# Starting the routed-expert stage in the middle of a shared-expert block

## The chip, the cores and the metric

The kernel runs on one core of a Trainium2 chip. The metric is the device time of one execution in microseconds. The engines are TensorE (PE in the profile, its weight loads PEld), VectorE (DVE), ScalarE (ACT), GpSimd (POOL) and SyncE (SP), which only issues DMAs.

## What is computed

4096 tokens (2 x 2048) of 512 features go through one layer: layer norm, a cross attention in which the scores are used only to pick 15 delays of the values, a residual, a second layer norm, and a feed-forward network with 16 experts of which each token uses 4, plus a shared expert of hidden width 1024. Only the feed-forward part is touched here:

```python
sg = xf @ shared_gate_w.T
su = xf @ shared_up_w.T
shared_out = silu(sg) * su @ shared_down_w.T
topk_idx, w, _ = _route(xf, router_w, correction_bias)      # 4 of 16 experts
combine = zeros((S, E)).at[arange(S)[:, None], topk_idx].add(w)
g = einsum('sc,ech->esh', xf, gate_w)
u = einsum('sc,ech->esh', xf, up_w)
hw = silu(g) * u * combine.T[:, :, None]
routed = einsum('esh,ehc->sc', hw, down_w)
return shared_out + routed
```

## The kernel before, in words

Every float32 matrix is split in a high and a low float16 part, and a product is three float16 products (high x high, high x low, low x high).

**The shared expert** works on 8 blocks of 512 tokens (four tiles of 128) and on 8 chunks of 128 hidden units, so there are 64 chunks, numbered g = 8 k + c for block k. A chunk is 24 matrix products of 512 columns for gate and up (`shared_half`, L948, or `gate_up_at`, L1137) and 12 for down (`shared_down`, L964, or `down_at`, L1149), which add up in four PSUM banks over the chunks of a block. Between them stand, per chunk, a silu on ScalarE (L1339, L1430), a product on VectorE from PSUM (L1623, L1961), the high part on ScalarE (L1345) and the low part on VectorE (L1629, L1966). The down products of a chunk come one chunk later in TensorE's order. After the last chunk of a block, VectorE adds the four PSUM banks to x1, the layer's residual (`shared_sum`, L1644, or `sum_at`, L1976); the down products of the next block wait for it.

**Stage A** runs chunks 0 to 39 (`FIRST = 5` blocks). Beside it the routing is worked out, the routed weights are split, and a list of tokens by expert is made: for each of the 32 tiles of tokens VectorE makes a one-hot of rows (L1858, one instruction for 4 experts) and four one-hots of blocks (L1861, one instruction each), in a ring of four buffers, and TensorE multiplies them (`tokens`, L980, four products a tile). The table `HOT` says which tiles belong to which of the chunks 26 to 37 (two or three each). The low parts of the 16 routed weights are made by GpSimd (`routed_weights_lo`, L2050 and L2051), one behind each conversion on ScalarE (`CONVERT`, L1351 to L1354), the last in chunk 37. When the token list is there (`s_tok`), GpSimd copies its first column (L2063) and begins to gather token rows (L2070).

**Stage B**, the routed experts, is a list of 143 blocks of 128 tokens of one expert. Its gate and up products are L1074, the turned hidden units L1088, the down products L1098, and each block's result goes to memory (`y_dram`). It begins with `turn_rows` (L1057) of the first two gathered blocks. Beside it SyncE saves x1 of block 4, loads x1 of block 5 and the turned rows of block 6 (the tables `OUT_AT`, `IN_AT`, `QUARTER_AT`).

**Stage C** runs chunks 40 to 63, and beside them the combination: for each of the 32 tiles GpSimd gathers 4 x 128 rows of `y_dram` (L2127, 128 gathers in a ring of four tiles, paced by `PACE`, 20 groups of 12 products for 37 gathers), VectorE multiplies and adds each (L1953, in the numbers of `PARTS_AT` per chunk) and SyncE writes the tile out. SyncE loads what the tiles need by the tables `OLD_IN`, `X1_IN` and `TURN_IN`; it takes its work strictly in order.

Of the kernel before, what the change touches and what calls it, by code (L numbers as in the profile page):

```python
# [26 lines left out]
F32 = mybir.dt.float32  # L27
# [5 lines left out]
P = 128  # L33
# [6 lines left out]
SH = HS // H  # L40
# [18 lines left out]
FIRST = 5  # L59
SPLIT = E // (FIRST - WITH)  # L60
# [22 lines left out]
RING = 4  # L83
PACE = (20, 37)
# [58 lines left out]
def build(nc, x, ctxT, wk, wqT, wv, wo, biases, bo, cb, routerT, gu_w, dn_w, const, const_r, out):  # L143
    with ExitStack() as ctx:
# [85 lines left out]
        old = [view(o + 8 * KB * (RING + k), [TB, D]) for k in range(FIRST)]  # L230
        xt_end = view(o + 88 * KB, [2 * KC, BLK], F16)
        x1_end = {FIRST: x1b, **{k: view(o + 8 * KB * (RING + k - 1), [TB, D]) for k in range(FIRST + 1, NB)}}
# [62 lines left out]
        x1s_dram = nc.dram_tensor("x1s_dram", [FIRST, P, TB, D], F32)  # L295
# [68 lines left out]
        s_hot, s_hot_used, s_tok = sem("one_hot_ready"), sem("one_hot_used"), sem("tokens_ready")  # L364
        s_token_now = sem("tokens_copied")
# [4 lines left out]
        s_xq = {k: sem(f"xt_quarters_in{k}") for k in (FIRST + 1, FIRST + 2)}  # L370
# [20 lines left out]
        for k, olds in enumerate(OLD):  # L391
            turns += [(FIRST + k, (FIRST + k) * TB + t) for t in range(TB)]
            turns += [(FIRST + k, m) for m in range(sum(OLD[:k]), sum(OLD[:k + 1]))]
        of_block = [[n for n, (k, m) in enumerate(turns) if k == FIRST + b] for b in range(len(OLD))]

        def result(m):

            return old[m // TB][:, m % TB, :] if m < FIRST * TB else x1_end[m // TB][:, m % TB, :]
# [16 lines left out]
        def gate_up_bank(s, n):  # L415

            return bank[(6 if isinstance(s, int) and s < 2 else 2) + n % 2]

# [10 lines left out]
        def _(sp):  # L429
# [200 lines left out]
            def x1s_tile_out(k, t):  # L630
                sp.wait_ge(s_x1s, TB * k + BANKS_FREE.index(t) + 1)
                sp.dma_start(x1s_dram[k][:, t, :], x1b[:, t, :]).then_inc(s_x1sw, 16)

            def x1_tile_in(k, t):
                sp.dma_start(x1b[:, t, :], x1_rows[k][:, t, :]).then_inc(s_x1i, 16)

# [6 lines left out]
            sp.wait_ge(s_sd, FIRST * SH)  # L643
            turn_fourth(1, 1)
            for s in range(BLOCKS):
# [3 lines left out]
                if s in OUT_AT:  # L649
                    x1s_tile_out(FIRST - 1, OUT_AT.index(s))  # L650
                if s in IN_AT:
                    if s == IN_AT[0]:
                        sp.wait_ge(s_x1sw, 16 * (FIRST - 1 + TB))
                    x1_tile_in(FIRST, IN_AT.index(s))
# [1523 lines left out]
```

## Time and profile before

| | us |
|---|---|
| time, median of 3 runs | 1013.74 (1006.69 to 1016.24) |
| the profiled execution's own time | 1004.85 |
| its span | 1003.0 |
| TensorE busy | 985.6 |
| VectorE busy | 660.1 |
| GpSimd busy | 437.1 |
| ScalarE busy | 380.6 |

The rows further down all come from the one profiled execution, whose own time is 1.85 us over its span and 8.9 us below the median of the runs. "Busy" of TensorE is the union of overlapping matrix products, so that a short pause between two of them doesn't show. A bracket at the end of a timeline row is the idle time ahead of it and what ended it; "issue" stands for nothing that the profile shows, "remote" for an unknown queue or another core.

### The profile page before, as it was taken

To read this page: it belongs to the slowest core of one execution; us is meant where nothing else is said; L and a number is where in the kernel's file an instruction comes from. 1 tells how busy PE (TensorE), PEld (TensorE's weight loads), DVE (VectorE), ACT (ScalarE), POOL (GpSimd) and SP (SyncE) were. 2 spreads that over 40 slices of the span, in tenths; PEclk is the share of its full clock that TensorE was granted. 3 is DMA by queue.
4 is the path that set the end of the run, shared out by engine and by line. 5 is a ranking of instruction groups with operands and counts; after the bars stand their busy time and mean duration, and the time that the engine had idled before them with its cause. 6 is when DMAs were issued, how large, how long until landed. Compare 5 with 4: busy or idle time off the path is not lost.

```text
span 1003.0 us, 21036 instructions
## 1 busy us (share of the span) xinstructions
PE 985.6 (98%) x6750; PEld 601.2 (60%) x6750; DVE 660.1 (66%) x1534; ACT 380.6 (38%) x776; POOL 437.1 (44%) x508
## 2 busy tenths in 40 slices
PE   9999999999999999999999999999999999999997
PEld 7776744444444444446787777878778744344442
DVE  4977688874588898875455554555545436676767
ACT  3646454433544333223444444444444411111111
POOL 0726422131145222134545444454454167776774
PEclk9999999999999999999999999999999999999999
DMA  9736858878463611416999999999888578988776
GB/s 347 259 121 206 293 182 233 227 206 237 156 179 99 200 62 63 144 35 178 265 269 256 271 267 256 255 269 249 243 242 252 173 210 267 309 272 283 242 239 219
DMA packets 176636, 219.02 MB, mean 218 GB/s; under 512 B 101225, under 2 KB 112361, under 8 KB 175529
## 3 DMA queue, kind: packets, MB, share of 16 engines
q1 hardware_dynamic: 152792, 139.05, 46.6%
q0 software_dynamic: 23760, 78.79, 26.0%
q8 instruction: 61, 1.00, 0.4%
q14 instruction: 23, 0.18, 0.1%
HBM read 124.72 MB, written 70.27 MB: 194 GB/s over the span
## 4 chain that ended last, share of the span: by engine, by line
PE 87%; DVE 5%; issue 3%; DMA 2%; ACT 2%; another core or an unknown queue 0%; POOL 0%; DVEq 0%; SPq 0%; ACTq 0%; POOLq 0%
PE bank L1074 19%; PE bank L948 18%; PE bank L1137 11%; PE bank L964 9%; PE bank L1098 9%; PE bank L1149 5%; PE bank L1057 5%; PE bank L723 2%; PE bank L703 2%; PE bank L1088 2%; PE bank L800 1%; DMA arena<-in_dn_w 1%; PE bank L980 1%; PE bank L713 1%; PE bank L807 1%
## 5 line engine op out<-in xcount | busy, mean ns | idle before, releaser
L948 PE MATMUL bank<-arena 128*128 128x512 f16 x960 | 218.1, 379 | 0.2 <-ACT arena L1330 0.2
L1074 PE MATMUL bank<-arena 128*128 x1716 | 211.2, 273 | 1.0 <-DVE arena L1615 0.8
L1074 PEld LDWEIGHTS bank<-arena 128*128 128x128 f16 x1716 | 162.9, 98 | 26.9 <-issue 2.0
L2070 POOL DMA_INDIRECT arena<-xr_dram,arena x143 | 140.7, 984 | 57.7 <-issue 45.9
L2127 POOL DMA_INDIRECT arena<-y_dram,arena x128 | 134.4, 1050 | 70.9 <-issue 32.9
L948 PEld LDWEIGHTS bank<-arena 128*128 128x128 f16 x960 | 94.2, 99 | 108.2 <-ACT arena L1330 0.7
L1137 PE MATMUL bank<-arena 128*128 128x512 f16 x576 | 129.2, 379 | 1.6 <-issue 1.5
L1098 PE MATMUL bank<-arena 128*128 x429 | 115.4, 378 | 0.5 <-ACT arena L1408 0.5
L1345 ACT ACTIVATE arena<-arena 128x512 f16<-128x512 f32 x64 | 40.3, 629 | 197.8 <-DVE arena L1623 96.0
L1890 DVE SCALAR_TENSOR_TENSOR arena<-bank,arena 128x128 f32<-128x128 f32 x143 | 41.6, 291 | 107.6 <-ACT arena L1397 82.8
L1953 DVE SCALAR_TENSOR_TENSOR arena<-arena 128x512 f32<-128x512 f32 x128 | 95.1, 750 | 25.4 <-DMA arena<-y_dram,arena 16.9
L964 PE MATMUL bank<-arena 128*128 128x512 f16 x480 | 110.1, 379 | 0.2 <-DVE arena L1629 0.2
L1137 PEld LDWEIGHTS bank<-arena 128*128 128x128 f16 x576 | 56.1, 98 | 71.0 <-issue 4.6
L2050 POOL TENSOR_TENSOR arena<-arena 128x1024 f32 x16 | 34.5, 2158 | 144.6 <-ACT arena L1354 144.6
L1397 ACT ACTIVATE arena<-bank 128x128 f32<-128x128 f32 x143 | 39.7, 278 | 142.8 <-PE bank L1074 92.1
L1408 ACT ACTIVATE arena<-bank 128x512 f32<-128x512 f32 x143 | 83.2, 582 | 2.9 <-PE bank L1098 1.7
L2063 POOL COPY arena<-arena 128x1 int32 (+1 forms) x143 | 28.4, 198 | 121.1 <-PE bank L1057 108.7
L964 PEld LDWEIGHTS bank<-arena 128*128 128x128 f16 x480 | 46.8, 98 | 56.5 <-DVE arena L1629 0.7
L1893 DVE TENSOR_TENSOR arena<-arena 128x128 f16<-128x128 f32 x143 | 41.9, 293 | 53.7 <-ACT arena L1401 47.7
L1615 DVE COPY arena<-bank 128x1024 f16<-128x1024 f16 x108 | 73.7, 682 | 5.0 <-issue 2.6
L1057 PEld LDWEIGHTS bank<-arena 128*128 128x128 f16 x864 | 57.1, 97 | 26.1 <-DMA arena<-xr_dram,arena 0.9
L1149 PE MATMUL bank<-arena 128*128 128x512 f16 x288 | 66.1, 379 | 5.6 <-DVE arena L1976 2.9
(226 smaller groups left out, 1281.7 us busy)
## 6 DMA issues: line engine op xcount, KB each, us to landing
y_dram<-arena SPq DMA_DIRECT2D x143, 256.0 KB
arena<-in_x SPq DMA_DIRECT2D x8, 1024.0 KB, 12.4
xr_dram<-arena SPq DMA_DIRECT2D x16, 512.0 KB, 3.8
x_dram<-arena SPq DMA_DIRECT2D x8, 1024.0 KB, 5.6
arena<-in_gu_w SPq DMA_DIRECT2D x16, 512.0 KB, 3.6
out<-arena SPq DMA_DIRECT2D x32, 256.0 KB
arena<-x_dram SPq DMA_DIRECT2D x5, 1024.0 KB
arena<-x1s_dram SPq DMA_DIRECT2D x20, 256.0 KB
```

The costliest lines, as they stand in the source:

```text
L948: last = mm(bank[half][:, :], (gu_hi_s, gu_lo_s)[wp][:, c, at:at + H], xt[:, xv * KC + kc, :], start=(n == 0), stop=(n == 3 * KC - 1))
L964: last = mm(bank[2 + t][:, :], s_hb[:, g % 2, hv, t * P:t * P + P], (dn_hi_s, dn_lo_s)[wp][:, c, :], start=(c == 0 and n == 0), stop=(c == ...
L1057: last = turn(bank16[p % 2][:, n * P:n * P + P], xg[:, s % 4, n * P:n * P + P], id16)
L1074: last = mm(gate_up_bank(s, s)[:, 0:2 * H], rows[:, xv * KC + kc, :], only((gu_hi_r, gu_lo_r)[wp], e, slice(kc * 2 * H, (kc + 1) * 2 * H)) ...
L1098: last = mm(bank[6 + j][:, :], r_hT[:, j, hv, :], only((dn_hi_r, dn_lo_r)[wp], e), start=(n == 0), stop=(n == 2))
L1137: last = mm(bank[GATE_UP[n % 2][g]][:, :], (gu_hi_s, gu_lo_s)[wp][:, c, at:at + H], xt[:, xv * KC + kc, :], start=(m == 0), stop=(m == 3 * ...
L1149: last = mm(bank[2 + t][:, :], s_hb[:, n % 2, hv, t * P:t * P + P], (dn_hi_s, dn_lo_s)[wp][:, c, :], start=(c == 0 and m == 0), stop=(c == ...
L1408: A(y_sb[n % 4], bank[6 + n % 2][:, :], ACT.Copy, scale=1.0 / WS).then_inc(s_ye, 1)
L1615: V.tensor_copy(xgT[:, j, :, :], bank16[j].rearrange("p (n q) -> p n q", n=2 * KC)).then_inc(s_txe, 1)
L1953: V.scalar_tensor_tensor(acc, ybuf[n % RING][:, e, :], w, acc, ALU.mult, ALU.add).then_inc(s_cmb, 1)
L2070: pool.indirect_dma_start(out=dst, out_offset=None, in_=xr_dram[:, :], in_offset=bass.IndirectOffsetOnAxis(ap=token_now[:, r:r + 1], axis= ...
L2127: pool.indirect_dma_start(out=ybuf[n % RING][:, e, :], out_offset=None, in_=y_dram[:, :], in_offset=bass.IndirectOffsetOnAxis(ap=row_of[:, ...
```

## The change

Stage A ends after chunk 36 of the count (chunks 0 to 35), in the middle of block 4, and stage C runs chunks 36 to 63. The half sum of block 4 is added to x1 at the end of stage A, stays in SBUF, and stage C starts its four banks afresh and adds the other half. Stage B no longer saves and loads x1 nor turns rows of block 6; the turned rows of blocks 6 and 7 and x1 of blocks 5 to 7 are loaded in stage C. The one-hots of the 32 tiles are made four tiles a chunk in chunks 26 to 33, and GpSimd makes two of the four block one-hots of each tile, with a semaphore of its own. The conversions of routed weights stand at other chunks, and GpSimd takes the low parts from a written list, behind its one-hots. The tables of stage C are new.

```diff
-FIRST = 5
+AHEAD = 36
+CUT = AHEAD // SH
-CONVERT = {15: 1, **{g: 1 for g in range(17, 24)}, **{g: 1 for g in (25, 26, 28, 29, 31, 32, 35, 37)}}
+CONVERT = {15: 1, **{g: 1 for g in range(17, 24)}, **{g: 1 for g in (24, 25, 26, 28, 29, 31, 33, 34)}}
-HOT = {26: (0, 3), 27: (3, 6), 28: (6, 9), 29: (9, 11), 30: (11, 14), 31: (14, 17), 32: (17, 19), 33: (19, 22), 34: (22, 25),
-       35: (25, 27), 36: (27, 30), 37: (30, 32)}
+HOT = {26 + n: (TB * n, TB * n + TB) for n in range(8)}
+BLOCKS_BY_POOL = 2
+LOW_BEHIND = {25: (8, 9), 26: (10,), 28: (11,), 29: (12,), 31: (13,), 33: (14, 15)}
-LAST = range(FIRST * SH, S // BLK * SH)
-OLD = (6, 7, 7)
-OUT_AT, IN_AT, QUARTER_AT = (10, 16, 22, 28), (36, 42, 48, 54), (60, 68, 76, 84)
-OLD_IN = {-1: (0, 1), 0: (2, 3), 1: (4, 5), 2: (6, 7), 7: (8, 9), 9: (10, 11), 11: (12, 13), 12: (14, 15), 16: (16, 17), 18: (18, 19)}
-X1_IN = {4: (24, 25), 5: (26, 27), 13: (28, 29), 14: (30, 31)}
-TURN_IN = (3, 6, 8, 10)
-PARTS_AT = (0, 4, *(6,) * 6, 4, *(6,) * 4, 4, 6, 6, 4, *(6,) * 6, 4)
-PACE = (20, 37)
+LAST = range(AHEAD, S // BLK * SH)
+OLD = (0, 5, 5, 6)
+OLD_IN = {0: (0, 1), 1: (2, 3), 4: (4, 5), 6: (6, 7), 10: (8, 9), 11: (10, 11), 18: (12, 13), 19: (14, 15)}
+X1_IN = {-1: (20, 21), 0: (22, 23), 7: (24, 25), 8: (26, 27), 15: (28, 29), 16: (30, 31)}
+TURN_IN = {6: (5, 6, 7, 9), 7: (12, 13, 14, 17)}
+PARTS_AT = (0, 5, 6, 5, 4, 4, 5, 6, 5, 4, 4, 5, 6, 5, 4, 4, 5, 6, 5, 4, 4, 5, 6, 5, 4, 4, 5, 3)
+PACE = (5, 8)
...
-                if n in (9, 13):
+                if n in (9, 15):
                     k = 2 if n == 9 else 3
                     x1s_out(k)
                     next_x1_in(k)
...
-                if s in OUT_AT:
-                    x1s_tile_out(FIRST - 1, OUT_AT.index(s))
-                if s in IN_AT:
...
-                if s in QUARTER_AT:
-                    quarter_turned_in(FIRST + 1, xtb_p[:, (FIRST + 1 - WITH) % 2, :, :], QUARTER_AT.index(s))
...
+                for k, moments in TURN_IN.items():
+                    if n in moments:
+                        if k < NB - 1:
+                            sp.wait_ge(s_su, SH * (k - 1))
+                        quarter_turned_in(k, turned_at(k), moments.index(n))
...
                     pe.wait_ge(s_hot, t + 1)
+                    pe.wait_ge(s_hot_p, t + 1)
...
             whole(pair_blk, pair_slot, -0.5 + 0.5 / P)
+            V.engine_nop().then_inc(s_picked, 1)
...
-                for e in range(TOP_E):
+                for e in range(TOP_E - BLOCKS_BY_POOL):
                     last = V.tensor_scalar(hot_blk[q][:, e, :], places16, pair_blk[:, t + e * T:t + e * T + 1],
                                            token_id[:, t:t + 1], ALU.is_equal, ALU.mult)
...
-            for first in (0, E // 2):
-                if first:
-                    pool.wait_ge(s_picked, 1)
-                with pool.Fori(first // 2, (first + E // 2) // 2) as i:
-                    for j in range(2):
-                        routed_weights_lo(2 * i + j, j)
+            def block_hots(t):
+
+                if t >= 4:
+                    pool.wait_ge(s_hot_used, t - 3)
+                for e in range(TOP_E - BLOCKS_BY_POOL, TOP_E):
+                    last = pool.tensor_scalar(hot_blk[t % 4][:, e, :], places16, pair_blk[:, t + e * T:t + e * T + 1],
+                                              token_id[:, t:t + 1], ALU.is_equal, ALU.mult)
+                last.then_inc(s_hot_p, 1)
+
+            with pool.Fori(0, E // 4) as i:
+                for j in range(2):
+                    routed_weights_lo(2 * i + j, j)
+            pool.wait_ge(s_picked, 1)
+            for g in range(25, AHEAD):
+                if g in HOT:
+                    pool.wait_ge(s_picked, 2)
+                    for t in range(*HOT[g]):
+                        block_hots(t)
+                for n in LOW_BEHIND.get(g, ()):
+                    routed_weights_lo(n, n % 2)
             pool.wait_ge(s_tok, 1)
```

## Rows read from the trace of the kernel before

**Rows 1.** The page: the span, and busy time by engine.
```profile
span 1003.0 us, 21036 instructions
PE 985.6 (98%) x6750; PEld 601.2 (60%) x6750; DVE 660.1 (66%) x1534; ACT 380.6 (38%) x776; POOL 437.1 (44%) x508
```
**Rows 2.** Busy time by stretch: PE, PEld, DVE, ACT, POOL, granted clock, DMA share, GB/s.
```profile
380.00:450.00 70.00, 70.00 (x385) 34.59 (x384) 57.50 (x129) 21.61 (x28) 18.53 (x17) 1.00 0.25 77
...
470.00:800.00 330.00, 329.80 (x3147) 261.56 (x3146) 169.99 (x514) 147.50 (x412) 154.65 (x262) 1.00 0.90 252
802.50:1003.00 200.50, 188.51 (x865) 83.75 (x863) 131.07 (x188) 29.71 (x49) 134.42 (x128) 0.99 0.82 255
```
**Rows 3.** Timeline of PE in stage C: start, us, what.
```profile
802.53 10.52 PE L1137 MATMUL bank<-arena 128*128 128x512 f16 x48
...
862.13 5.34 PE L1137 MATMUL bank<-arena 128*128 128x512 f16 x24
...
869.90 3.21 PE L1137 MATMUL bank<-arena 128*128 128x512 f16 x12
...
879.73 2.75 PE L1149 MATMUL bank<-arena 128*128 128x512 f16 x12 [2.92 <-DVE arena L1976]
...
990.86 2.75 PE L1149 MATMUL bank<-arena 128*128 128x512 f16 x12
995.48 2.76 PE L1149 MATMUL bank<-arena 128*128 128x512 f16 x12 [1.87 <-DVE arena L1966]
```
**Rows 4.** Groups of VectorE from 802.5 us on: count, busy, mean ns, idle before.
```profile
L1953 DVE SCALAR_TENSOR_TENSOR arena<-arena 128x512 f32<-128x512 f32 x128 | 95.1, 750 | 25.4 <-DMA arena<-y_dram,arena 16.9 <-issue 6.1
...
L1961 DVE SCALAR_TENSOR_TENSOR arena<-bank,arena 128x512 f32<-128x512 f32 x24 | 16.5, 687 | 39.3 <-remote 24.4 <-PE bank L1137 10.4 <-ACT arena L1430 3.8
```
**Rows 5.** Groups of GpSimd over the whole run.
```profile
L2127 POOL DMA_INDIRECT arena<-y_dram,arena x128 | 134.4, 1050 | 70.9 <-issue 32.9 <-DMA y_dram<-arena 18.2 <-remote 15.7
...
L2063 POOL COPY arena<-arena 128x1 int32 (+1 forms) x143 | 28.4, 198 | 121.1 <-PE bank L1057 108.7 <-PE bank L964 6.7 <-DVE arena L1872 4.1
```
**Rows 6.** Timeline of PE at the end of stage A and the start of stage B.
```profile
431.92 2.75 PE L964 MATMUL bank<-arena 128*128 128x512 f16 x12
...
440.44 2.75 PE L964 MATMUL bank<-arena 128*128 128x512 f16 x12
443.03 0.66 PE L980 MATMUL bank<-arena 128*128 128x144 f16 x8
443.53 5.34 PE L948 MATMUL bank<-arena 128*128 128x512 f16 x24
...
451.30 1.06 PE L1057 MATMUL bank<-arena 128*128 128x128 f16 x16
```
**Rows 7.** Timeline of VectorE there.
```profile
417.98 1.00 DVE L1861 TENSOR_SCALAR arena<-arena 128x144 f16<-128x144 f16 x4
418.89 0.68 DVE L1858 TENSOR_TENSOR arena<-arena 128x512 f16<-128x512 f16 x1
419.49 3.80 DVE L1861 TENSOR_SCALAR arena<-arena 128x144 f16<-128x144 f16 x4
...
444.23 6.03 DVE L1875 SCALAR_TENSOR_TENSOR arena<-arena 128x144 f32<-128x144 f32 x15
```
**Rows 8.** Timelines of GpSimd and ScalarE there.
```profile
419.99 2.14 POOL L2050 TENSOR_TENSOR arena<-arena 128x1024 f32 x1 [20.93 <-ACT arena L1354]
422.09 1.15 POOL L2051 TENSOR_TENSOR arena<-arena 128x512 f32 x1
...
444.11 0.54 POOL L2063 COPY arena<-arena 128x1 int32<-128x1 int32 x2 [4.07 <-DVE arena L1872]
```
```profile
435.03 1.48 ACT L1354 ACTIVATE arena<-arena 128x1536 f32<-128x1536 f32 x1
```
**Rows 9.** Timeline of SyncE and VectorE before the first wait of rows 3.
```profile
868.21 1.45 SPq L638 DMA_TRANSPOSE arena<-xr_dram  x1
```
```profile
863.61 1.54 DVE L1953 SCALAR_TENSOR_TENSOR arena<-arena 128x512 f32<-128x512 f32 x2 [3.99 <-DMA arena<-y_dram,arena]
```

More of the change, by code:

```diff
@@ L229, in build @@
         ybuf = [view(o + 8 * KB * r, [TOP_E, D]) for r in range(RING)]
-        old = [view(o + 8 * KB * (RING + k), [TB, D]) for k in range(FIRST)]
+        old = [view(o + 8 * KB * (RING + k), [TB, D]) for k in range(CUT)]
         xt_end = view(o + 88 * KB, [2 * KC, BLK], F16)
-        x1_end = {FIRST: x1b, **{k: view(o + 8 * KB * (RING + k - 1), [TB, D]) for k in range(FIRST + 1, NB)}}
+        x1_end = {CUT: x1b, **{k: view(o + 8 * KB * (RING + k - 1), [TB, D]) for k in range(CUT + 1, NB)}}
         o4 = o3 + 12 * KB
@@ L391, in build @@
         for k, olds in enumerate(OLD):
-            turns += [(FIRST + k, (FIRST + k) * TB + t) for t in range(TB)]
-            turns += [(FIRST + k, m) for m in range(sum(OLD[:k]), sum(OLD[:k + 1]))]
-        of_block = [[n for n, (k, m) in enumerate(turns) if k == FIRST + b] for b in range(len(OLD))]
+            turns += [(CUT + k, (CUT + k) * TB + t) for t in range(TB)]
+            turns += [(CUT + k, m) for m in range(sum(OLD[:k]), sum(OLD[:k + 1]))]
+        of_block = [[n for n, (k, m) in enumerate(turns) if k == CUT + b] for b in range(len(OLD))]
         def result(m):
-            return old[m // TB][:, m % TB, :] if m < FIRST * TB else x1_end[m // TB][:, m % TB, :]
+            return old[m // TB][:, m % TB, :] if m < CUT * TB else x1_end[m // TB][:, m % TB, :]
         block = ctx.enter_context(nc.Block())
@@ L642, in _ @@
             turn_fourth(0, 0)
-            sp.wait_ge(s_sd, FIRST * SH)
+            sp.wait_ge(s_sd, AHEAD)
             turn_fourth(1, 1)
@@ L964, in shared_down @@
                         last = mm(bank[2 + t][:, :], s_hb[:, g % 2, hv, t * P:t * P + P], (dn_hi_s, dn_lo_s)[wp][:, c, :],
-                                  start=(c == 0 and n == 0), stop=(c == SH - 1 and n == 2))
+                                  start=(c == 0 and n == 0), stop=((c == SH - 1 or g == AHEAD - 1) and n == 2))
                 last.then_inc(s_sd, 1)
@@ L989, in next_attention @@
                 attention(n, t, 6)
-            for g in range(FIRST * SH):
+            for g in range(AHEAD):
                 k, c = g // SH, g % SH
@@ L1149, in down_at @@
                         last = mm(bank[2 + t][:, :], s_hb[:, n % 2, hv, t * P:t * P + P], (dn_hi_s, dn_lo_s)[wp][:, c, :],
-                                  start=(c == 0 and m == 0), stop=(c == SH - 1 and m == 2))
-                    if n == LAST[-1]:
-                        last.then_inc(s_fin, 1)
-                if n < LAST[-1]:
-                    last.then_inc(s_sd, 1)
+                                  start=(first and m == 0), stop=(c == SH - 1 and m == 2))
+                    if t == TB - 1 or n == LAST[-1]:
+                        last.then_inc(s_sd, 1)
             pe.wait_ge(s_txe, on_tensor(BLOCKS - 1) + 1)
@@ L1356, in _ @@
             converted = 0
-            for g in range(FIRST * SH):
+            for g in range(AHEAD):
                 if g - 1 in ROUTE:
@@ L1869, in _ @@
                     one_hots(t)
-            chunk(38)
+            chunk(AHEAD - 2)
             dve.wait_ge(s_hot_used, T)
@@ L1879, in _ @@
             V.engine_nop().then_inc(s_expert, 1)
-            chunk(39)
+            chunk(AHEAD - 1)
             def hidden(s, n):
@@ L1983, in _ @@
                 hidden_at(n, parts[:ahead])
-                if c == 0 and k > FIRST:
+                if c == 0:
                     sum_at(k - 1)
```

74 lines of the change are left out of this document (33 added, 41 removed).

## The prediction

> **What bounds the kernel now.** I read the page's busy times first, then busy time by stretch, then TensorE's timeline wherever a stretch is not full, and last who it waited for there. TensorE is busy 985.6 of 1003.0 us [rows 1], so all that any change of order can take away is the other 17.4 us, 1.7%. The stretches say where they are: the end of stage A and the bulk of stage B have TensorE at 70.00 of 70 and at 329.80 of 330 us at full granted clock, stage C at 188.51 of 200.5 [rows 2]. So stage C holds some 12 of the 17.4.
>
> Stage C against its own rate: one chunk, 36 products, repeats every 7.77 us (862.13 to 869.90 [rows 3]). 24 chunks would be 186.5 us. From 802.53 to the end of the last product, 995.48 + 2.76 = 998.24, it is 195.7 [rows 3]. Lost: 9.2 us. Two places make up most of it. At the border of blocks 5 and 6 the products due at 869.90 + 5.18 = 875.08 start at 879.73 (4.65 lost, 2.92 of it waiting for VectorE's block sum). At the end the last 12, due at 990.86 + 2.59 = 993.45, start at 995.48 (2.03 lost, waiting for VectorE's low part) [rows 3]. Some 2.5 us are short gaps. What makes VectorE late is that gathers are late (16.9 us of waiting) and that TensorE's signals reach it late ("remote", 24.4 us) [rows 4]. The gathers are late because GpSimd is nearly full: (134.4 + 70.9 - 18.2) / 128 = 1.46 us for each [rows 5], where the pace asks for one every 20 x 2.59 / 37 = 1.40 us. 998.24 to 1003.0, the last sums and writes, 4.8 us, is not touched.
>
> **The change part by part.**
>
> 1. *Four chunks move from stage A to stage C.* TensorE's products are the same in number (64 x 36), of one form, and at the same rate in both stages (431.92 to 443.53 is 8.52 + 2.59 + the 0.50 of 8 token products; 8.52 less 12 such products, 0.75, is 7.77 too [rows 6]). Cost 0. The half sum adds four VectorE instructions of 0.62, 2.5 us once; hidden, since TensorE doesn't wait for block 4's second half to be summed until a chunk later.
>
> 2. *Stage C gets wider.* The pace becomes 5 x 2.59 / 8 = 1.62 us per gather, over the 1.46 that GpSimd needs, so gathers no longer fall behind. VectorE has 131.07 us in 24 chunks, 5.46 each of 7.77 [rows 2]. After: 131.07 + 4 x 2 x 0.69 + 2.5 = 139.1 in 28, 4.97 each. In the last chunk 3 combinations stand, not 4, and the one before has 5. So a late signal is made up within a chunk. I take both named waits as gone, 2.92 + 2.03 = 4.95 us, and the 1.7 us of gaps next to the first and the 2.5 elsewhere as staying, since nothing in the change touches them. Bounds: 0 (the lateness of signals is what counts, and it isn't removed) and 9.2 (all of it follows from the load). What is late next is the border at chunk 40, new; its sum waits for 16 combinations, which are done by then.
>
> 3. *SyncE's work moves.* 8 copies of x1 and 4 transposed loads leave stage B. TensorE idles 0.2 us there in 330 [rows 2], so at most 0.2 is won; I take 0. Copies in stage C: 4 fewer old tiles, 4 more of x1, equal; and 4 more transposed loads. Such a load at 868.21 stood right before the late border, and a gather was late by 3.99 us shortly before it [rows 9]. With 7.77 - 4.97 = 2.8 us of slack a chunk I take 0; the upper bound is one border like the old one, 4.65. The transposes of block 6 wait for the products of chunk 39, long past at tile turn 5. SyncE keeps queued behind them only writes and loads with tables of their own.
>
> 4. *The last weights and the start of stage B.* Now let u be the start of the down products in the chunk before the last of stage A (440.44). ScalarE's conversion in the chunk before ended at 435.03 + 1.48 = 436.51, 4.6 us after that chunk's 431.92 [rows 6, 8]. In the changed kernel conversion 15 stands in chunk 34, the last but one, so it ends at u + 4.6, and GpSimd's low part takes 2.14 + 1.15 = 3.3 [rows 8] until u + 7.9. Behind it in GpSimd's queue stand the token copy and the first gathers: before, the copy began at u + 3.67 (444.11), now at u + 8.0, 4.3 us later. The other side is VectorE. While GpSimd reads SBUF, VectorE stands: the four block one-hots take 1.00, but 3.80 where they meet L2050 and L2051, and they end with these [rows 7, 8]. The 15 steps that count blocks (L1875, 6.03 us from u + 3.8 [rows 7]) have two SBUF inputs and now meet the low part: up to 3.3 later, and the products behind `turn_rows` wait for VectorE. TensorE comes to `turn_rows` at 451.30, u + 10.86 [rows 6], now 0.5 later for 8 more token products in that chunk. Upper bound 4.3 + the latency not yet shown, say 5; lower 0, if the landing before had that much slack. I take 3.0, near the lock's 3.3.
>
> 5. *One-hots, four tiles a chunk, half the block ones on GpSimd.* Per chunk of 7.77 + 16 x 0.0625 = 8.77 us VectorE has 1.37 for the hidden units and 4 x (0.60 + 2 x 0.23) = 4.24 (0.60 and 0.91 / 4 from the distances of starts [rows 7]). GpSimd has 8 one-hots of P and, in four of the eight chunks, a low part of 3.3, mean 1.65. If every GpSimd microsecond stops VectorE, save the about 1.3 in which VectorE waits for ScalarE or reads PSUM, the chunk is full at 8 P + 1.65 = 8.77 - 5.61 + 1.3, P = 0.35 us. No row shows P. From below: the copy of one column, 0.20 [rows 5]. From above: 1.15, the subtraction of 512 columns [rows 8]. Between the two subtractions a column costs (2.14 - 1.15) / 512 = 1.93 ns, so 144 cost 0.17 + 0.28 = 0.45; a form with one tensor input should be less. I take 0.40: 8 x 0.05 x 8 = 3.2 us too much, less about 2 that the ring of four tiles can hold back before TensorE waits. Cost 1.5. At 0.20, 0; at 0.6, part B below.
>
> This is also where the Trainium skill bears on the case. "SBUF — State Buffer", section "Who interferes with whom", has the port pair of VectorE and GpSimd as a lock held for the whole instruction, taken by `tensor_scalar` in its fast modes and, against a GpSimd read, by instructions with two SBUF inputs. By that rule, the 3.80 against 1.00 agrees, and work given to GpSimd is not taken off VectorE but put in its way, at more than the 0.23 saved. "GPSIMD Engine Reference", section "Elementwise — side-by-side cycle accounting", gives 1.8 to 2.6 cycles at 1.2 GHz for an element, an estimate of 0.22 to 0.31 us for 144 before dispatch; the sum would be the same by it, as it lies about the threshold.
>
> **Sum.** -4.95 + 0 + 0 + 3.0 + 1.5 = -0.45 on the profiled execution, 1004.85 to 1004.4. The median of the runs lies 8.9 us above that execution. No trace shows where; if it is spread as the profiled losses are, about half, 4.5, is in stage C, and half of that goes as half of 9.2 does: -2.25. 1013.74 - 0.45 - 2.25 = 1011.0 us.
>
> **The rivals.**
>
> A. *Stage C gives up nearly all, and the start of stage B hides behind the counting.* All late gathers and waits vanish (-8.2, leaving 1), steps 4 and 5 cost 0, and the 4.5 of the other runs go too: 1013.74 - 12.7 = 1001.0. For it: gathers behind pace explain most of VectorE's named waits [rows 4, 5]. Against: gaps marked issue and late signals are not GpSimd's doing.
>
> B. *The port is the bound in chunks 26 to 33.* At P = 0.6, 8 x 0.25 = 2.0 us a chunk, 16 in eight, less 3 held by the ring: 13. In place of the 1.5: 1011.0 + 11.5 = 1022.5, slower. The Trainium skill's page named in step 5 is the rule that stands behind this rival. It decides from P = 0.35 on, and outweighs the gain at about 0.45. For it: 3.80 against 1.00 [rows 7]. Against: TensorE had no gap in 70 us with the same meetings before [rows 2].
>
> C. *The transposes take back what the pace gives.* Eight in stage C, three of each four one tile apart, delay gathers by 4 us [rows 9] and one border waits 4.65 again: 1011.0 + 4.65 = 1015.6, no change.
>
> D. *The change doesn't do what it says:* the pace was never what held VectorE, the signals were; step 2 is 0 and steps 4 and 5 stand: 1013.74 + 4.5 = 1018.2.
>
> **How the numbers follow.** Forecast 0.46, A 0.24, B 0.11, C 0.12, D 0.07. A measurement of this kernel tells about 1% (10 us) from no change. Faster by over 1% is below 1003.6: all of A but a little, and the rim of the forecast, 0.25. Slower is above 1023.9: most of B's upper part, 0.08. The rest, 0.67, is no change. The range runs from A's 1001.0 to just short of B, 1021: about 0.2 is outside.
>
> **What would show it.** Step 2: stage C's 28 chunks at 7.77 are 217.6 us; right if first product to last end takes 221 to 223. No wait of over 1 us for L1976 or the last low part, and gathers idle between pairs. Step 4: the token copy comes some 8 us after u, `turn_rows` waits for a gather or for VectorE, and about 3 us pass without products. Step 5: P itself, the mean of the new GpSimd group, and gaps ahead of L980 or L948 in chunks 27 to 34; wrong if there are none at P over 0.45 or many below 0.3. Step 3: gathers late right behind a transpose. The forecast is wrong if TensorE's idle time falls below 10 us or grows beyond 25.

## The result: slower by 1%

The changed kernel takes 1020.32 us (median of 20 runs, 1013.66 to 1026.72), the kernel before, on the same chip, 1010.35 (20 runs, 1004.70 to 1016.24). The ratio is 1.0099, 95% interval 1.0076 to 1.0123. The forecast, 1011.0 and "no change" on balance, had the wrong sign: it lay 0.3% under the 1013.74 that it started from, and the kernel moved up by 1.0%. The time lies at the upper rim of the range. Of the variant e2 below, three executions over 1.5% above its fastest on the same chip are in the medians and not in the ratios.

The profiled execution of the changed kernel takes 1021.63 us, its span is 1019.8. The page, against [rows 1]:

```profile
span 1019.8 us, 21030 instructions
PE 997.1 (98%) x6750; PEld 607.5 (60%) x6750; DVE 647.1 (63%) x1474; ACT 380.5 (37%) x776; POOL 502.4 (49%) x572
```

TensorE's busy time grew by 11.5 us with the same number of products, so part of the loss isn't idle time: some products ran at half clock. The stretches, in the columns of [rows 2]:

```profile
380.00:450.00 70.00, 62.17 (x356) 32.10 (x354) 51.21 (x100) 20.13 (x27) 63.01 (x59) 0.94 0.39 98
...
798.40:1016.10 217.70, 217.70 (x1009) 98.51 (x1007) 138.69 (x199) 34.95 (x57) 134.28 (x128) 1.00 0.80 235
97.00:125.00 28.00, 26.56 (x175) 18.01 (x174) 16.68 (x31) 11.04 (x15) 13.49 (x14) 0.76 0.77 265
```

The last column but two is the granted clock. In stage C TensorE was busy for 188.51 of 200.5 us before and is now busy for all of 217.70. The end of stage A, 70.00 of 70 before, now has 7.8 us without products, with GpSimd busy for 63 of 70. The stretch 97 to 125 has a clock of 0.76. The kernel before has 1.00 there:

```profile
97.00:125.00 28.00, 27.44 (x222) 19.19 (x221) 20.42 (x41) 13.03 (x18) 13.49 (x14) 1.00 0.84 291
```

The change touches no code there. Cutting both executions at places of TensorE's timeline gives the ledger (from start of a product to start of a product):

| stretch of TensorE's timeline | before | after | difference |
|---|---|---|---|
| start to the first token product (L980, now L973) | 350.1 | 357.4 | +7.3 |
| first to last start of a token product | 93.4 (12 chunks), lost 0 | 74.4 (8 chunks), lost 12.1 over the 62.3 of 7 x 8.77 + 0.94 | +12.1 |
| last gate product of stage A to first of stage B (L1074, now L1067) | 4.4 | 9.7 | +5.3 |
| its first 12 gate and 12 down products | 4.0 | 6.2 | +2.2 |
| stage C, first gate to last down product | 195.3, lost 9.1 | 217.3 = 28 x 7.77 less one product, lost 0 | -9.1 |
| end of the last down product to the end of the span | 4.8 | 3.7 | -1.0 |

Without the first line it is 12.1 + 5.3 + 2.2 - 9.1 - 1.0 = +9.5, and the medians differ by 10.0. The first line is no part of the change: over the thirteen profiled executions of all kernels here this place came at 350.1 to 364.4 us, in the three of one and the same kernel (e2 below) at 351.1, 357.9 and 364.4. Most of the difference is a stretch of lower granted clock in the first 125 us. So variants are compared below by the time from the first token product to the end of the span as well, which leaves it out: 652.9 before, 662.4 after.

Where TensorE waited, in the changed kernel (total, times, longest), the first two groups:

```profile
PE bank L973 <- POOL arena L2052: 7.9, 5, 2.3
PE bank L1050 <- DMA arena<-xr_dram,arena: 5.2, 2, 4.0
```

Before, L1149 waited 2.92 and 1.87 us for VectorE [rows 3]; these waits are gone. L2052 is the new one-hot on GpSimd. TensorE's timeline at these waits:

```profile
360.64 0.41 PE L973 MATMUL bank<-arena 128*128 128x144 f16 x4 [2.19 <-POOL arena L2052]
...
370.73 0.41 PE L973 MATMUL bank<-arena 128*128 128x144 f16 x4 [1.41 <-POOL arena L2052]
372.84 0.64 PE L973 MATMUL bank<-arena 128*128 128x144 f16 x4 [1.70 <-POOL arena L2052]
373.27 6.78 PE L940 MATMUL bank<-arena 128*128 128x512 f16 x24
...
383.48 5.34 PE L940 MATMUL bank<-arena 128*128 128x512 f16 x24
...
443.73 0.61 PE L1050 MATMUL bank<-arena 128*128 128x128 f16 x8 [3.97 <-DMA arena<-xr_dram,arena]
445.55 1.01 PE L1050 MATMUL bank<-arena 128*128 128x128 f16 x8 [1.22 <-DMA arena<-xr_dram,arena]
446.52 2.74 PE L1067 MATMUL bank<-arena 128*128 x12
449.06 3.85 PE L956 MATMUL bank<-arena 128*128 128x512 f16 x12
...
453.19 1.47 PE L1067 MATMUL bank<-arena 128*128 x12
```

Several of the stalls do their damage twice. After 1.41 and 1.70 us of waiting the next 24 gate and up products take 6.78 us, after a chunk without a wait the same 24 take 5.34. After 3.97 and 1.22, 12 gate products take 2.74; a block later, 1.47. Some products run at the lower of the clock's two levels, 1.2 GHz. Not every stall has that: behind the 2.19 us of 360.64 the next 24 took 5.34, full clock.

Why GpSimd is late, in its own timeline:

```profile
351.30 9.20 POOL L2052 TENSOR_SCALAR arena<-arena 128x144 f16<-128x144 f16 x8
360.46 2.46 POOL L2043 TENSOR_TENSOR arena<-arena 128x1024 f16<-128x1024 f32 x1
362.88 1.16 POOL L2044 TENSOR_TENSOR arena<-arena 128x512 f16<-128x512 f32 x1
364.02 15.83 POOL L2052 TENSOR_SCALAR arena<-arena 128x144 f16<-128x144 f16 x16
...
437.85 0.66 POOL L2070 COPY arena<-arena 128x1 int32<-128x1 int32 x2
```

and in the groups of GpSimd (count, busy, mean ns, idle before):

```profile
L2052 POOL TENSOR_SCALAR arena<-arena 128x144 f16<-128x144 f16 x64 | 66.1, 1045 | 0.3 <-PE bank L973 0.3
```

P is 1.045 us in the mean. Eight of them, 8.4, and a low part of 3.3 make 11.7 us in a chunk of 8.77 that has a low part; over eight chunks the one-hots and the four low parts are 80.0 us against 70.2. From 351.30 to 431.28 GpSimd stands for 0.3 us in all: it is the bound there. But the mean hides two prices. VectorE beside it:

```profile
356.21 0.53 DVE L1854 TENSOR_SCALAR arena<-arena 128x144 f16<-128x144 f16 x2
...
360.86 3.23 DVE L1854 TENSOR_SCALAR arena<-arena 128x144 f16<-128x144 f16 x2
...
380.14 0.69 DVE L1615 SCALAR_TENSOR_TENSOR arena<-bank,arena 128x512 f32<-128x512 f32 x1 [5.41 <-issue]
```

and GpSimd's one-hots as a group (shortest/median/longest in ns), in the middle of VectorE's, and while VectorE stands for 5.41 us:

```profile
L2052 POOL TENSOR_SCALAR arena<-arena x64: 837/920/1856, 351.3 to 430.3; 128x144 f16<-128x144 f16 x64
```
```profile
354.77 2.30 POOL L2052 TENSOR_SCALAR arena<-arena 128x144 f16<-128x144 f16 x2
```
```profile
374.88 4.97 POOL L2052 TENSOR_SCALAR arena<-arena 128x144 f16<-128x144 f16 x6
```

At 360.86, against the subtractions L2043 and L2044, VectorE's two one-hots take 3.23. At 356.21, while GpSimd is in the middle of its one-hots, the same two take 0.53: a one-hot on GpSimd hardly holds VectorE, a subtraction does. The other way it is GpSimd that loses. Its one-hots take 0.84 us each while VectorE stands (4.97 for six) and 1.15 beside VectorE's one-hots (2.30 for two). Of all 64, the 12 with nothing on VectorE beside them take 0.837 to 0.841, the 8 beside nothing but its product from PSUM (L1615) the same, and the 31 beside its one-hots 1.24 in the mean. At 0.84 throughout, GpSimd would have had 53.7 + 13.9 = 67.6 us of work in the 70.2, an estimate: it would just have fitted. So meeting VectorE is part of the price. That this causes the longer times is read from which instructions lie side by side; no run separates it.

The Trainium skill's page "SBUF — State Buffer", section "Who interferes with whom", gives the shared port pair as a lock held for a whole instruction, by the engine that issues first. The 3.23 agrees, with VectorE as the one that waits; the 0.84 against 1.24 fits it with GpSimd as the one that waits. Why VectorE's one-hots never wait for GpSimd's (0.53) no run here shows.

### The profile page after: what moved, and what is told of

Its sections match the earlier page's. It is cut to its first block, busy times and chain, and to the rows that moved or that the text cites. A ratio compares the mean times of both kernels' runs of the same rounds, so it can differ in the third digit from the quotient of the medians.

```text
span 1019.8 us, 21030 instructions
## 1 busy us (share of the span) xinstructions
PE 997.1 (98%) x6750; PEld 607.5 (60%) x6750; DVE 647.1 (63%) x1474; ACT 380.5 (37%) x776; POOL 502.4 (49%) x572
## 4 chain that ended last, share of the span: by engine, by line
PE 79%; POOL 7%; DVE 7%; issue 3%; ACT 2%; DMA 1%; another core or an unknown queue 0%; DVEq 0%; SPq 0%; ACTq 0%; POOLq 0%
PE bank L1067 18%; PE bank L1130 14%; PE bank L940 11%; PE bank L1091 9%; PE bank L1143 7%; PE bank L956 5%; POOL arena L2052 5%; PE bank L1050 5%; PE bank L1081 2%; PE bank L715 1%; POOL arena L2043 1%; PE bank L792 1%; PE bank L695 1%; DVE arena L1568 1%; PE bank L729 1%
## 5 line engine op out<-in xcount | busy, mean ns | idle before, releaser
L1067 PE MATMUL bank<-arena 128*128 x1716 | 212.3, 274 | 0.5 <-DVE arena L1607 0.4
L940 PE MATMUL bank<-arena 128*128 128x512 f16 x864 | 203.5, 388 | 1.4 <-DMA arena<-pt_dram 1.2
L1067 PEld LDWEIGHTS bank<-arena 128*128 128x128 f16 x1716 | 163.5, 98 | 26.8 <-issue 1.6
L1130 PE MATMUL bank<-arena 128*128 128x512 f16 x672 | 149.5, 379 | 0.0
L1946 DVE SCALAR_TENSOR_TENSOR arena<-arena 128x512 f32<-128x512 f32 x128 | 95.7, 750 | 31.8 <-DMA arena<-y_dram,arena 29.4
L956 PE MATMUL bank<-arena 128*128 128x512 f16 x432 | 100.2, 382 | 0.2 <-DVE arena L1621 0.2
L1143 PE MATMUL bank<-arena 128*128 128x512 f16 x336 | 76.9, 379 | 0.0
L1050 PE MATMUL bank<-arena 128*128 128x128 f16 x864 | 66.3, 219 | 5.6 <-DMA arena<-xr_dram,arena 5.2
```

What stands on the lines that cost most here:

```text
L940: last = mm(bank[half][:, :], (gu_hi_s, gu_lo_s)[wp][:, c, at:at + H], xt[:, xv * KC + kc, :], start=(n == 0), stop=(n == 3 * KC - 1))
L956: last = mm(bank[2 + t][:, :], s_hb[:, g % 2, hv, t * P:t * P + P], (dn_hi_s, dn_lo_s)[wp][:, c, :], start=(c == 0 and n == 0), stop=((c = ...
L1050: last = turn(bank16[p % 2][:, n * P:n * P + P], xg[:, s % 4, n * P:n * P + P], id16)
L1067: last = mm(gate_up_bank(s, s)[:, 0:2 * H], rows[:, xv * KC + kc, :], only((gu_hi_r, gu_lo_r)[wp], e, slice(kc * 2 * H, (kc + 1) * 2 * H)) ...
L1130: last = mm(bank[GATE_UP[n % 2][g]][:, :], (gu_hi_s, gu_lo_s)[wp][:, c, at:at + H], xt[:, xv * KC + kc, :], start=(m == 0), stop=(m == 3 * ...
L1143: last = mm(bank[2 + t][:, :], s_hb[:, n % 2, hv, t * P:t * P + P], (dn_hi_s, dn_lo_s)[wp][:, c, :], start=(first and m == 0), stop=(c == ...
```

## The experiments

**First question: is it GpSimd's own time, the density of four tiles a chunk, or the width of the one-hot?** Four kernels on one chip, where the kernel before took 1009.32. The changed kernel did not run beside them, so it is set against them by its ratio and its trace.

*e1_no_pool*, VectorE makes all block one-hots again:

```diff
-BLOCKS_BY_POOL = 2
+BLOCKS_BY_POOL = 0
-                    pe.wait_ge(s_hot_p, t + 1)
...
-                        block_hots(t)
```

> The changed kernel, but VectorE makes all four block one-hots of a tile. Theory 1 (GpSimd's own time: 64 one-hots of 1.045 us, 8.4 a chunk and a low part of 3.3 beside, against a chunk of 8.8): the waits for the GpSimd one-hots (7.9 us) and the half-clock products behind them (about 4) go, and the last low part is not behind, so that of the 7.5 us lost at the start of stage B some 4 go too: 1020.3 - 12 - 4 = about 1004, range 1001 to 1009. Theory 2 (four tiles a chunk are too many for any engine: VectorE then has 1.4 + 4 x 1.5 = 7.4 of 8.8, and 3.3 more behind the port in four chunks): the waits move to VectorE's one-hots, 6 us or more of them stay, and the time is 1010 to 1018.

1022.92 us (4 runs), ratio to before 1.0126 (1.0068 to 1.0185); first token product to end 662.6. TensorE's waits:

```profile
PE bank L972 <- DVE arena L1853: 8.3, 8, 2.5
PE bank L1049 <- DMA arena<-xr_dram,arena: 6.9, 3, 5.3
```

The wait has only changed hands. VectorE's four tiles take about 6.0 us a chunk, with 1.37 for the hidden units 7.4 of 8.77, and the low parts push it over:

```profile
386.11 3.84 DVE L1853 TENSOR_SCALAR arena<-arena 128x144 f16<-128x144 f16 x4
```

Against a low part four one-hots take 3.84 us, otherwise 0.99. So taking GpSimd's one-hots away wins nothing by itself, and the theory that they alone are the cause falls. The other theory has the waits right and the time too low. The start of stage B was longer still, 11.4 us: ScalarE waited 6.8 us for VectorE (L1614) ahead of the last conversion, and the last low part waited for that.

*e2_one_by_pool*, one block one-hot of four on GpSimd:

```diff
-BLOCKS_BY_POOL = 2
+BLOCKS_BY_POOL = 1
```

> The changed kernel with one of four block one-hots on GpSimd. Theory 1: GpSimd has 4 x 1.05 = 4.2 a chunk and 3.3 more in four of eight, 7.5 at most, under the chunk's 8.8, so TensorE waits for it no more; the time is within 2 us of the kernel with none, about 1004 to 1006. If instead each GpSimd one-hot costs VectorE its own length through the shared port, the loss halves only: about 1014.

1007.46 us (10 runs), ratio 0.9987 (0.9949 to 1.0024); on two other chips 1.0042 (1.0011 to 1.0074) and 0.9956 (0.9916 to 0.9996). First token product to end: 652.1.

```profile
PE bank L1050 <- DMA arena<-xr_dram,arena: 3.9, 3, 2.4
PE bank L973 <- DVE arena L1854: 2.1, 1, 2.1
```
```profile
L2052 POOL TENSOR_SCALAR arena<-arena 128x144 f16<-128x144 f16 x32 | 39.5, 1244 | 14.0 <-PE bank L973 13.9
```

One digit gives back what the change had lost; the time is a little over the 1004 to 1006 expected. The idle time of 14.0 ahead of GpSimd's one-hots says that it now waits for the ring and not the ring for it; token products take 66.3 us instead of 74.4, and stage B's start 8.1 instead of 9.7. Each of GpSimd's one-hots takes 1.24 us in the mean here, since nearly all of them meet VectorE's. The three ratios of one kernel differ by 0.9%, and it is the kernel before that moves with the chip: the fastest execution with a granted clock of 0.998 or more was 1002.1, 1001.1 and 1003.2 us for e2 on the three chips, and 1004.9, 994.5 and 1007.0 for the kernel before. So ratios from different chips can't be set against each other at this size. Why the kernel before is 10 us faster on the second chip stays open; it was not profiled there.

*e3_before_two_by_pool*, the kernel before, with two of the four block one-hots on GpSimd:

```diff
+BLOCKS_BY_POOL = 2
+LOW_BEHIND = {25: (8,), 26: (9,), 28: (10,), 29: (11,), 31: (12,), 32: (13,), 35: (14,), 37: (15,)}
...
-                for e in range(TOP_E):
+                for e in range(TOP_E - BLOCKS_BY_POOL):
```

> The kernel before with two of four block one-hots on GpSimd, two or three tiles a chunk as before. Theory 1: GpSimd has 6 x 1.05 = 6.3 and 3.3 in chunks with three tiles and a low part, 9.6 of 8.5, but chunks without one between them: it falls behind by 1 us at a time and the ring holds that: 0 to 3 us over the kernel before, and the last low part a little later: 1010 to 1014. If a GpSimd one-hot as such is the price, whatever the density, it is 12 us over: 1022.

1014.61 us (8 runs), ratio 1.0052 (1.0028 to 1.0076). Waits and the GpSimd group:

```profile
PE bank L1153 <- DVE arena L1971: 5.0, 1, 5.0
PE bank L1153 <- issue: 3.9, 1, 3.9
...
PE bank L984 <- POOL arena L2064: 0.5, 1, 0.5
```
```profile
L2064 POOL TENSOR_SCALAR arena<-arena 128x144 f16<-128x144 f16 x64 | 65.5, 1034 | 8.0 <-PE bank L984 7.8
```

The same 64 one-hots of the same mean, 1.03 us, spread over twelve chunks, make TensorE wait 0.5 us in place of 7.9. What cost 12 us is thus the product of price and density. The time itself rose by 5.3 us, over the 0 to 3 expected; of the 4.2 by which its profiled execution is longer than the one before, 3.4 lie in stage C (198.7 for 195.3), in code that it doesn't touch.

*e4_half_width*, each one-hot on GpSimd cut in two of 72 columns:

```diff
-                    last = pool.tensor_scalar(hot_blk[t % 4][:, e, :], places16, pair_blk[:, t + e * T:t + e * T + 1],
-                                              token_id[:, t:t + 1], ALU.is_equal, ALU.mult)
+                    for c in range(0, COLUMNS, COLUMNS // 2):
+                        half = slice(c, c + COLUMNS // 2)
+                        last = pool.tensor_scalar(hot_blk[t % 4][:, e, half], places16[:, half],
+                                                  pair_blk[:, t + e * T:t + e * T + 1],
+                                                  token_id[:, t:t + 1], ALU.is_equal, ALU.mult)
```

> The changed kernel with each GpSimd one-hot of 144 columns cut in two of 72, 128 instructions. It measures what the 1.045 us are. If they are columns, one takes about 0.6 and all take 77 us, little more than the 66 before; the time rises by about 10. If they are a fixed cost of the form, one takes about 1.0, all take 128 us, and the time rises by some 60.

1044.44 us in one run.

```profile
PE bank L973 <- POOL arena L2054: 24.0, 12, 3.3
```
```profile
L2054 POOL TENSOR_SCALAR arena<-arena 128x72 f16<-128x72 f16 x128 | 92.1, 740 | 0.1
```
```profile
L2054 POOL TENSOR_SCALAR arena<-arena x128: 600/607/1637, 348.9 to 453.6; 128x72 f16<-128x72 f16 x128
```

In the mean 72 columns cost 0.740 and 144 cost 1.045, but both means hold one-hots that met VectorE's. By the shortest, 0.600 and 0.837, a column costs (0.837 - 0.600) / 72 = 3.3 ns and the fixed part is 0.36 us, an estimate from two points. Neither of the two expectations holds: it is both columns and a fixed part. The prediction had taken 1.93 ns a column and 0.17 us from the two subtractions. GpSimd's extra 26.0 us became 27.2 us more from the first to the last token product (101.6 against 74.4 in the changed kernel): it is the bound there, one for one.

**Second question: stage B's start, and what emptied stage C of waits.** Three variants of e2 on another chip, where the kernel before took 1001.66 and e2 again 1004.02.

> The kernel with one block one-hot of four on GpSimd once more, on the same chip as the next three, as their base: 1007.5 plus or minus 3.

*e5_weights_early*, the last conversions and low parts two chunks earlier:

```diff
-... for g in (24, 25, 26, 28, 29, 31, 33, 34)}}
+... for g in (24, 25, 27, 28, 29, 30, 31, 32)}}
-LOW_BEHIND = {25: (8, 9), 26: (10,), 28: (11,), 29: (12,), 31: (13,), 33: (14, 15)}
+LOW_BEHIND = {25: (8,), 26: (9,), 27: (10,), 28: (11,), 29: (12,), 30: (13,), 31: (14,), 32: (15,)}
```

> One block one-hot of four on GpSimd, and the eight last routed weights converted at chunks 24, 25 and 27 to 32, each low part behind that chunk's one-hots, so that the last is done in chunk 32. Theory 1 (the start of stage B is late because the last low part stands ahead of the first gathers in GpSimd's queue): the token copy follows the token list at once, as in the kernel before, the waits for gathered rows at the start of stage B (3.9 us with one one-hot on GpSimd) fall below 0.5, the half-clock products behind them go, and the time is 4 to 5 us under that kernel's 1007.5: about 1003. Rival: VectorE's count of blocks or the landing of the gathers holds TensorE anyway, and the gain is under 1 us. A risk that would show as waits for VectorE's one-hots: low parts in six chunks in a row.

1010.83 us (6 runs), ratio 1.0094 (1.0057 to 1.0130): not 4 to 5 us under e2, as expected, but above its 1004.02. The start of stage B fell to 4.3 us, as before the change, so step 4's cause is shown: the low parts ahead of the first gathers in GpSimd's queue. The edit takes them off VectorE's port at that place too, but the waits that went are those for gathered rows. A low part in nearly every one-hot chunk costs there:

```profile
PE bank L973 <- DVE arena L1854: 7.0, 9, 0.9
```
```profile
392.97 2.70 DVE L1854 TENSOR_SCALAR arena<-arena 128x144 f16<-128x144 f16 x3
...
396.19 1.60 DVE L1854 TENSOR_SCALAR arena<-arena 128x144 f16<-128x144 f16 x3
...
398.32 0.76 DVE L1854 TENSOR_SCALAR arena<-arena 128x144 f16<-128x144 f16 x3
```
```profile
393.44 2.18 POOL L2043 TENSOR_TENSOR arena<-arena 128x1024 f16<-128x1024 f32 x1 [1.06 <-ACT arena L1346]
395.58 1.71 POOL L2044 TENSOR_TENSOR arena<-arena 128x512 f16<-128x512 f32 x1
```

Three one-hots take 0.76 alone, 2.70 and 1.60 where they meet L2043 and L2044. Here rival B's port decides as B has it: with only one of four block one-hots on GpSimd, VectorE is the one late, and by the subtractions. From the first token product to the end this run took 650.6, 2.3 less than the kernel before, and 0.7 less than e2 on this chip (651.3), while its ratio says 9 us more than before. Part of that is the kernel before, which is faster on this chip (above). Why e5 and e2 lie 6.8 us apart in their medians, with ratio intervals that overlap, while their traces differ by so little, stays open.

*e7_pace_only*, e5 with the old pace of the gathers, and *e6_packed_tail*, e7 with the old packing of VectorE's combinations as well:

```diff
-PACE = (5, 8)
+PACE = (20, 37)
```
```diff
-PARTS_AT = (0, 5, 6, 5, 4, 4, 5, 6, 5, 4, 4, 5, 6, 5, 4, 4, 5, 6, 5, 4, 4, 5, 6, 5, 4, 4, 5, 3)
+PARTS_AT = (0, 4, *(6,) * 6, 4, *(6,) * 4, 4, 6, 6, 4, *(6,) * 6, 4, 0, 0, 0, 0)
```

> The same, but only the pace of the gathers is the old one (1.40 us each); the combinations per chunk are the new ones. If VectorE's load per chunk made the losses of stage C, none come back, 1003; if the gathers' rate and their DMA traffic did, 3 us or more come back.

> As the kernel with the weights early, but stage C is packed as before: a gather every 1.40 us and VectorE's combinations six a chunk, so that the last four of the 28 chunks have none. Theory 1 (stage C lost 9 us because each chunk was nearly full of gathers and combinations): its losses come back, 4 to 9 us, and the time is that much over the kernel it is made from, about 1009. Theory 2 (it lost them by chance signals or by the last chunk's work alone, which stays empty here): within 2 us of it.

e7: 1010.75 us (7 runs), ratio 1.0085 (1.0055 to 1.0116), stage C 217.3 with nothing lost. e6: 1019.37 (4 runs), ratio 1.0170 (1.0112 to 1.0228), stage C 227.4. Both lie some 8 us above the times expected, since e5 does; e6 is 8.5 over e5, within the 4 to 9 of its first theory. Of e6, TensorE and then VectorE:

```profile
865.89 4.15 PE L1143 MATMUL bank<-arena 128*128 128x512 f16 x12 [2.60 <-DVE arena L1959]
...
902.57 4.44 PE L1143 MATMUL bank<-arena 128*128 128x512 f16 x12 [4.04 <-DVE arena L1969]
```
```profile
864.48 0.75 DVE L1946 SCALAR_TENSOR_TENSOR arena<-arena 128x512 f32<-128x512 f32 x1 [5.99 <-DMA arena<-y_dram,arena]
865.15 0.68 DVE L1959 TENSOR_TENSOR arena<-arena 128x512 f16<-128x512 f32 x1
```

The pace alone costs nothing in stage C. With six combinations a chunk VectorE comes to a gather that isn't there, stands 5.99 us, and the low part L1959 behind it is late for TensorE. The 12 down products after the waits of 2.60 and 4.04 take 4.15 and 4.44 us in place of 2.75: half clock again. So the loss in stage C comes back with the packing, 10.1 us of it, and goes with the spread of `PARTS_AT` over four more chunks, at the old pace too (e7). The losses of the kernel before look to be of the same kind [rows 3, 4], VectorE's combinations running up against the gathers in its own queue. Whether the slower pace alone, with the old packing, would take them away as well wasn't run. In the changed kernel VectorE still waits 29.4 us for gathers, and nobody waits for it:

```profile
L1946 DVE SCALAR_TENSOR_TENSOR arena<-arena 128x512 f32<-128x512 f32 x128 | 95.7, 750 | 31.8 <-DMA arena<-y_dram,arena 29.4
```

**Third question: is there a version that keeps both gains?** Both are e2 with the last two conversions a chunk earlier and the last two low parts a chunk apart; e9 has no chunk with two low parts. On a third chip, before at 1013.72, e2 at 1011.71.

```diff
# e8_last_two_early
-... for g in (24, 25, 26, 28, 29, 31, 33, 34)}}
+... for g in (24, 25, 26, 28, 29, 31, 32, 33)}}
-LOW_BEHIND = {25: (8, 9), 26: (10,), 28: (11,), 29: (12,), 31: (13,), 33: (14, 15)}
+LOW_BEHIND = {25: (8, 9), 26: (10,), 28: (11,), 29: (12,), 31: (13,), 32: (14,), 33: (15,)}
# e9_one_low_each
+... for g in (24, 25, 27, 28, 29, 31, 32, 33)}}
+LOW_BEHIND = {25: (8,), 26: (9,), 27: (10,), 28: (11,), 29: (12,), 31: (13,), 32: (14,), 33: (15,)}
```

> The kernel with one block one-hot on GpSimd and the changed kernel's own table of weights, but the last two conversions at chunks 32 and 33 instead of 33 and 34, each low part behind its chunk's one-hots. Theory 1 (two causes apart: the last low part ahead of the first gathers costs 4 to 5 us at the start of stage B; a low part in each chunk costs VectorE's port): from the last gate product of stage A to the first of stage B it takes 4.4 us as in the kernel before, not 8 to 9, and the one-hot chunks wait at most 2 us more than with the old table. Time 2 to 4 us under the kernel with the old table, ratio to the kernel before about 0.997 to 1.001. Rival: low parts at 31, 32, 33 in a row stall VectorE by 0.9 each, and nothing is won.

> As that one, but a single low part behind each of chunks 25 to 29 and 31 to 33, so that no chunk has two. Port theory: the first wait of 2.1 us and its half-clock products (1.7), which follow the two low parts of chunk 25, go; but five low parts in a row bring waits of 0.9 a chunk from the third or so on. About even with the other: within 2 us.

> The kernel with one block one-hot on GpSimd and the changed kernel's table of weights, as the base of these two on the same chip: ratio to the kernel before 0.999 to 1.004.

e8: 1007.97 us (12 runs), ratio 0.9932 (0.9900 to 0.9965). e9: 1011.60 (12 runs), 0.9962 (0.9922 to 1.0002). Of e8:

```profile
364.93 0.42 PE L973 MATMUL bank<-arena 128*128 128x144 f16 x4 [2.10 <-DVE arena L1854]
365.19 5.34 PE L940 MATMUL bank<-arena 128*128 128x512 f16 x24
...
438.32 0.62 PE L1050 MATMUL bank<-arena 128*128 128x128 f16 x8 [0.89 <-DVE arena L1615]
439.38 1.62 PE L1067 MATMUL bank<-arena 128*128 x12 [0.43 <-issue]
```

No wait for gathered rows, and behind the short wait of 0.89 the 12 gate products take 1.62 us, not 2.74. Token products take 67.0 us, the start of stage B 5.5, and the time from the first token product to the end is 649.4, 3.5 less than before and 13.0 less than the changed kernel. The first stall, 2.10 us, has 24 products at full clock behind it (5.34); in e2's trace the same stall of 2.10 has 7.03. So the half clock behind a stall of this length comes and goes with the execution.

e9 did as the port theory says: the first wait is gone, there are five of up to 0.9 (4.1 us in all) with no half clock behind them, and 649.9 us from the first token product to the end. Its ratio touches 1.

The repeats of e2 came out lower than expected of them, 1004.02 and a ratio of 0.9956. The ratio of e8 to before is below 1 on this chip with its whole interval; 3.5 us is the smaller end of that interval. Against e2 on the same chip it is 0.9932 / 0.9956 = 0.998, and the two intervals overlap, so that e8 beats e2 is carried by the traces (649.4 against 652.1) and not by the times. With e2 about level with before over three chips, 0.2 to 0.4% is my estimate of what e8 gains.

## Why the prediction was wrong, point by point

**Step 1** (moved chunks cost 0): right; 28 chunks at 7.77 us each.

**Step 2** (stage C gives back 4.95 of 9.2): right in kind, mis-sized by 4.2. The whole loss went, a little more than rival A has it. I kept the gaps marked issue and the late "remote" signals as losses of their own. They went with the named waits; the first of them stands ahead of the 2.92, at the same late border, in the kernel before:

```profile
873.50 1.02 PE L1137 MATMUL bank<-arena 128*128 128x512 f16 x4 [0.39 <-issue]
```

The mechanism was off in one point: not the pace of the gathers (e7) but the density of VectorE's combinations (e6 against e7). Of rival D, "the pace was never what held VectorE" is thus borne out, its price of 0 for step 2 is not.

**Step 3** (SyncE's moves cost 0): right. Rival C is out: eight transposes in stage C, no product late.

**Step 4** (+3.0 for the start of stage B): the mechanism holds by e5, the size doesn't. Expected were the token copy at u + 8.0 and 3.0 us; it came at 437.85, u + 9.6 with u = 428.23, since GpSimd was behind in its own queue, and the cost was 5.3 of waiting and 2.2 of half clock, 7.5. In e2, where GpSimd is not behind, the copy came at u + 7.9 and the start was 3.7 longer than before, near the forecast; what the step left out were the backlog and the clock. The products waited for gathered rows; the counting steps on VectorE did not come last.

**Step 5** (+1.5 at P = 0.40): this is the step that failed. P is 1.045, close to the upper bound of 1.15 that I had drawn from the 512-column subtraction, and the cost was 12.1. Three things were wrong in it. The value came from a slope between two subtractions and the belief that "a form with one tensor input should be less"; e4 shows 3.3 ns a column for 1.93 and a fixed part of 0.36 us for 0.17, so 0.84 us for a one-hot that meets nothing. Contention was taken the wrong way round: the sum has every GpSimd microsecond stop VectorE, while in the trace VectorE's one-hots beside GpSimd's take their usual time and GpSimd's go from 0.84 to 1.24. And the threshold of 0.35 was VectorE's; 8 P + 3.3 against the chunk of 8.77 for GpSimd alone was never set, which gives P = 0.68 in a chunk with a low part. By GpSimd's own mean of 8 P + 1.65, P at its upper bound is 2.1 us over a chunk and 16.6 over eight, less 3 for the ring about 14: that sum would have made a loss of this size the main case. (The working itself also slips: 3.2 less 2 is 1.2, not 1.5.) **Rival B** had the place and nearly the price (13), with a chance of 0.11. Its mechanism is half right: the port counts, but in the kernel as changed it is GpSimd that is late; VectorE is late once GpSimd has only one of the four block one-hots and a low part in nearly every chunk (e5).

**Not in the sum at all**: the clock. Of the 12.1, 7.9 are waits, and products at half clock behind some of them are about 3.3 of the rest (1.44 and 1.36 in two sets of 24, 0.23 in each of two sets of token products); then come the 2.2 of stage B. The sign named at the end, TensorE's idle time outside 10 to 25 us, was blind to it: idle time was 1019.8 - 997.1 = 22.7 us, inside, with the forecast wrong, since products at half clock count as busy.

**The shift of -2.25 for the other runs** was wrong. I spread the 8.9 us between the profiled execution and the median over the losses that the trace shows. With 20 runs in place of 3 the median is 1010.35 and the distance 5.5. By the ledger the first 125 us, in code that has nothing to do with the change, are where executions differ most. Left out, the sum of the terms as measured, -9.1 + 7.5 + 12.1 = 10.5, and -1.0 behind the last product, which I had called untouched, make 9.5, against the 10.0 by which the medians differ.

## What to carry to other kernels

An operation that moves to another engine has to be priced by a row of its own form there, and where none exists, by the dearest neighbour, with that engine's whole queue for the stretch summed beside it; the sum that was missing here was a division, work per chunk by time per chunk, on GpSimd alone. Contention has to be asked for in both directions: the trace of the changed kernel has the moved instruction at 0.84 us alone and 1.24 beside VectorE's. A list of work that is spread thinner over more chunks frees the engine's queue for the instruction that the bottleneck waits for, even where the total is the same; a slower pace of the transfers is not needed for it. A stall of TensorE of some 2 us is to be counted with products at half clock that may come behind it: from nothing to about 2 us more here, and about 3.3 us behind 7.9 us of waits for one-hots in the changed kernel.

## What the runs showed of the hardware that was not expected

- A two-operation `tensor_scalar` on GpSimd, float16 with two operands taken per partition, takes 0.84 us for 144 columns and 0.60 for 72 (128 partitions) when nothing runs on VectorE, 1.045 and 0.740 in the mean of these kernels, while VectorE's takes 0.23 to 0.25. The Trainium skill, "GPSIMD Engine Reference", section "Elementwise — side-by-side cycle accounting", would give an estimate of 0.22 to 0.31 us for 144 columns before dispatch; the measured 3.3 ns a column is about 0.47 us for 144, and the measurement decides.
- VectorE's one-hots are held up by GpSimd's subtractions (3.23 us for two) but not by GpSimd's one-hots (0.53 for two); GpSimd's one-hots are held up by VectorE's (0.84 us alone, 1.24 in the mean beside them).
- In the first 125 us of some executions TensorE's granted clock is down for a stretch: 0.76 from 97 to 125 us in the changed kernel and in the second profile of e2, 1.00 in the kernel before and the first profile of e2, 0.89 from 0 to 97 in e8. The first token product came up to 12 us later with it in these, and 14 in the third profile of e2, which has 0.91 and 0.83 in the two stretches. The runs without a profile fit: within each kernel the time falls as the mean granted clock of the execution rises, by about 9 us from 0.990 to 1.000 for the kernel before. A wait for the load of `pt_dram` stood ahead of it in the changed kernel (1.21 us), but the profile of e3 has the same wait (1.03) and no loss. What sets it off stays open. That a variant makes it more frequent the record does not show: on the second chip the median granted clock was 0.992 for the kernel before and 0.996, 0.992 and 0.993 for e2, e5 and e7.
